# State-space block and ternary feed-forward on eight cores: 1024-wide weights cast through SBUF during the first layer norm, and the large casts issued ahead of it

## The reference, cut to what matters

```python
xn  = layernorm(x)                                   # x: 16 x 2048 x 1024, float32
xB  = einsum('bsd,nd->bsn', xn, B)                   # 128 states
state = tanh(state @ A.T + xB[:, t])                 # scan over 2048 steps
y   = einsum('bsn,dn->bsd', states, C) + D * xn + xn
attn = layernorm(y) * gamma + beta
h   = silu((xn @ w1.T) * s1) * ((xn @ w2.T) * s2)    # w1, w2: 4096 x 1024
h   = gelu((h @ h1.T) * h1s)                         # h1, h2: 4096 x 4096
h   = gelu((h @ h2.T) * h2s)
out = x + attn + (h @ w3.T) * w3s                    # w3: 1024 x 4096
```

## Time and profile before

| what | value |
|---|---|
| timed runs | 7653.4 and 8165.0 us, median 7909.2 us |
| the profiled execution, its own time | 7534.3 us |
| span of the profiled execution, slowest core | 7532.7 us |
| spans of the eight cores | 7508.8 to 7532.7 us |
| TensorE busy | 5344.8 us, 71% of the span |
| VectorE, ScalarE, GpSimd busy | 14%, 11%, 5% |
| mean granted TensorE clock | 0.93 |

### The profile page before, as it was taken

One profiled execution on the slowest core, in us unless ns is written; L12 is line 12 of the kernel. 1 busy time (PEld: TensorE's weight loads), 2 busy tenths in 40 slices (PEclk: granted clock), 3 DMA queues, 4 the chain that ended last, 5 costly groups with the idle time before them and its releaser, 6 DMA issues.

```text
span 7532.7 us, 63314 instructions; the slowest of 8 cores (7508.8 to 7532.7 us)
## 1 busy us (share of the span) xinstructions
PE 5344.8 (71%) x24252; PEld 2413.4 (32%) x24252; DVE 1079.8 (14%) x2367; ACT 815.4 (11%) x1621; POOL 372.3 (5%) x265
## 2 busy tenths in 40 slices
PE   3300004677916799779968996899699969986995
PEld 2200001233402344334433443344244424432442
DVE  4400002211093200210021003000300030012001
ACT  0000001222100100111011001110110010001010
POOL 0000000000001100110010001000200020001002
PEclk9999999899957899899989998999899989998997
DMA  1499993222323344334433443344344334433442
GB/s 54 78 111 109 109 108 74 73 96 95 140 87 109 123 151 151 118 123 151 151 112 134 151 151 106 134 151 149 103 145 151 138 114 146 151 129 115 151 151 92
DMA packets 185101, 919.75 MB, mean 122 GB/s; under 512 B 20836, under 2 KB 22117, under 8 KB 108264
## 3 DMA queue, kind: packets, MB, share of 16 engines
q1 hardware_dynamic: 158872, 739.53, 28.2%
q0 software_dynamic: 21328, 159.39, 14.0%
q10 hardware_dynamic: 4608, 16.78, 0.7%
HBM read 991.12 MB, written 109.05 MB: 146 GB/s over the span
## 4 chain that ended last, share of the span: by engine, by line
PE 57%; POOL 4%; DVE 3%; DMA 3%; issue 2%; ACT 0%; SPq 0%; DVEq 0%; POOLq 0%; ACTq 0%
PE pG L550 21%; PE pH L550 20%; PE pA L494 5%; PE pB L500 4%; PE pG L610 3%; PE pH L610 3%; DMA l1ring<-w2b 2%; POOL t1b L367 1%; POOL t2b L370 1%; POOL t1b L373 1%; POOL t2b L355 1%; PE pA L419 1%; DVE xnbt L430 1%; DVE t1b L358 1%; DVE t1b L350 0%
## 5 line engine op out<-in xcount | busy, mean ns | idle before, releaser
L550 PE MATMUL pG<-hbuf,hring 128*128 128x512 bf16 x4096 | 924.7, 382 | 5.5 <-DVE hbuf L464 3.7
L494 PE MATMUL pA<-xnbt,l1ring 128*128 128x512 bf16 x2048 | 566.0, 426 | 503.8 <-DVE hbuf L464 410.6
L550 PE MATMUL pH<-hbuf,hring 128*128 128x512 bf16 x4096 | 912.5, 379 | 2.3 <-issue 1.4
L550 PE MATMUL pG<-g1buf,hring 128*128 128x512 bf16 x4096 | 906.8, 379 | 8.0 <-ACT g1buf L528 7.8
L550 PE MATMUL pH<-g1buf,hring 128*128 128x512 bf16 x4096 | 906.8, 379 | 1.0 <-ACT hbuf L528 0.8
L419 PE MATMUL pA<-eye_s,xn_tm 128*128 128x128 f32 x256 | 57.0, 392 | 827.4 <-DVE xn_tm L407 827.4
L550 PEld LDWEIGHTS pG<-g1buf,hring 128*128 128x128 bf16 x4096 | 398.7, 98 | 490.0 <-issue 13.0
L550 PEld LDWEIGHTS pG<-hbuf,hring 128*128 128x128 bf16 x4096 | 398.8, 98 | 487.4 <-issue 26.2
L550 PEld LDWEIGHTS pH<-g1buf,hring 128*128 128x128 bf16 x4096 | 399.5, 98 | 481.3 <-issue 2.5
L550 PEld LDWEIGHTS pH<-hbuf,hring 128*128 128x128 bf16 x4096 | 395.7, 98 | 472.5 <-issue 5.4
L500 PE MATMUL pB<-xnbt,l1ring 128*128 128x512 bf16 x2048 | 519.7, 400 | 0.0
(11 more groups left out here) (91 smaller groups left out, 2401.4 us busy)
## 6 DMA issues: line engine op xcount, KB each, us to landing
hring<-h1b SPq DMA_DIRECT2D x256, 1024.0 KB, 5.0
hring<-h2b SPq DMA_DIRECT2D x256, 1024.0 KB, 5.1
l1ring<-w1b SPq DMA_DIRECT2D x256, 256.0 KB, 2.7
l1ring<-w2b SPq DMA_DIRECT2D x256, 256.0 KB, 2.9
hring<-w3b SPq DMA_DIRECT2D x64, 1024.0 KB, 5.5
xrb<-x POOLq DMA_DIRECT2D x96, 512.0 KB, 4.5
h1b<-h1t POOLq DMA_DIRECT2D x1, 32768.0 KB, 474.2
h2b<-h2t POOLq DMA_DIRECT2D x1, 32768.0 KB, 783.1
```

Of the source, the lines that this page charges most:

```text
L494: op("tensor", lambda e, p=pa, s=sl1, kk=k: e.matmul(p[:, 0:512], l1slot(s)[:, kk * 128:(kk + 1) * 128], xnbt[:, kk * 512:(kk + 1) * 512], ...
L550: op("tensor", lambda e, p=pg_, s=hs, kk=k, r=rsrc: e.matmul(p[:, 0:512], hslot(s)[:, kk * 128:(kk + 1) * 128], r[:, kk * 512:(kk + 1) * 512],
```

## The change

Three things are altered.

1. The DMAs that cast h1, h2 and w3 move from behind the phase 1 loop in GpSimd's stream to a place ahead of it, so they come before the loop's loads of `x`.
2. The DMAs that cast w1 and w2 are gone. In their place `emit_w12cast(u)` handles one of 64 pieces of 128 x 1024: SyncE loads the float32 piece to one of two halves of a new buffer `wcin`, VectorE casts it to `wcout`, and SyncE stores that to `w1b` or `w2b`. Each of the 32 iterations of the phase 1 loop ends with two such pieces.
3. SyncE's first loads from `w1b` and `w2b` wait for the 64 stores, in place of the two cast DMAs.

```diff
+        wcin = sb1("wcin", [128, 2 * 1024], F32)
+        wcout = sb1("wcout", [128, 2 * 1024], BF16)
...
         CV0_ALL = cv0.n
+
+        CSEM = {"h1": clC, "h2": clD, "w3": cv}
+        for nm_, s_, d_ in (("h1", h1t_d, h1b_d), ("h2", h2t_d, h2b_d),
+                            ("w3", w3t_d, w3b_d)):
+            op("gpsimd", lambda e, ss=s_, dd=d_: e.dma_start(dd, ss), CSEM[nm_], 16)
+
+        def emit_w12cast(u):
+            w_src = w1t_d if u < 32 else w2t_d
+            w_dst = w1b_d if u < 32 else w2b_d
+            mm_ = u % 32
+            slot = u % 2
+            ssem = cs if u < 32 else csB
+            wait("sync", cv0, CV0_CONSTS)
+            wait("sync", cl, u - 1)
+            ldn = dop("sync", lambda e, s=w_src[mm_],
+                      d=wcin[:, slot * 1024:(slot + 1) * 1024]: e.dma_start(d, s),
+                      wlc1 if slot == 0 else wlc2)
+            wait("vector", wlc1 if slot == 0 else wlc2, ldn)
+            if u >= 2:
+                wait("vector", cs if (u - 2) < 32 else csB,
+                     ((u - 2) + 1) * 16 if (u - 2) < 32 else ((u - 2) - 32 + 1) * 16)
+            cn = op("vector", lambda e, sl=slot: e.tensor_copy(
+                wcout[:, sl * 1024:(sl + 1) * 1024],
+                wcin[:, sl * 1024:(sl + 1) * 1024]), cl)
+            wait("sync", cl, cn)
+            dop("sync", lambda e, d=w_dst[mm_], sl=slot: e.dma_start(
+                d, wcout[:, sl * 1024:(sl + 1) * 1024]), ssem)
+
 
         for i in range(32):
...
             gset("pB0", (xb, xb.n))
+            emit_w12cast(2 * i)
+            emit_w12cast(2 * i + 1)
 
         gset("sqtmp", (v0b, v0b.n))
-        CSEM = {"w1": cl, "w2": clB, "h1": clC, "h2": clD, "w3": cv}
-        for nm_, s_, d_ in (("w1", w1t_d, w1b_d), ("w2", w2t_d, w2b_d),
-                            ("h1", h1t_d, h1b_d), ("h2", h2t_d, h2b_d),
-                            ("w3", w3t_d, w3b_d)):
-            op("gpsimd", lambda e, ss=s_, dd=d_: e.dma_start(dd, ss), CSEM[nm_], 16)
...
                 if tj == 0 and m == 0:
-                    wait("sync", cl, 16)
-                    wait("sync", clB, 16)
+                    wait("sync", cs, 32 * 16)
+                    wait("sync", csB, 32 * 16)
```

More of the change, by code:

```diff
@@ L136, in _build @@
                  "mmH", "scH", "mmW", "vW", "mmC2", "vC2", "mmT3",
-                 "v3", "x3", "x4", "mmF", "v7", "vout", "sout", "sdbg", "vsc", "p7")
+                 "v3", "x3", "x4", "mmF", "v7", "vout", "sout", "sdbg", "vsc", "p7", "wlc1", "wlc2")
         SM = {n: Sem(es.enter_context(nc.semaphore(n))) for n in names}
@@ L141, in _build @@
          sc2, v5b, wl, wlB, wh, mmL, scL, vL, mmH, scH, mmW, vW, mmC2,
-         vC2, mmT3, v3, x3, x4, mmF, v7, vout, sout, sdbg, vsc, p7) = (
-            SM[n] for n in names)
+         vC2, mmT3, v3, x3, x4, mmF, v7, vout, sout, sdbg, vsc, p7,
+         wlc1, wlc2) = (SM[n] for n in names)
         sbT = lambda n, shp, dt: es.enter_context(nc.sbuf_tensor(n, shp, dt))
```

## The result

The changed kernel is slower by 1.5%: the ratio to the kernel before is 1.015, with a 95% interval of 1.0099 to 1.0201. The interval excludes no change; whether 2% is reached it leaves open. Its timed runs have a median of 7669.3 us (7646.4 to 8173.2, 11 runs), those of the kernel before 7722.1 us (7533.7 to 8165.0, now 10 runs). The profiled execution took 7652.6 us, against 7534.3 before. The prediction said 7647 us.

What follows compares the result with a forecast made beforehand. It took VectorE's 751 us wait for `x`, behind five casts on GpSimd's queue, as the bound. +670.7 (later loop), +192 (pieces) and -750 (wait) gave +112.7 us on 7534.3: 7647 us, range 7580 to about 7830.

Steps and rivals of the forecast that it cites:

- The loop's start: Phase 1 loop, behind the casts and the constants: first instruction at 725 us, between 710 and 750.
- The casts: h1, h2 and w3 first in GpSimd's queue: 709 us, plus 8 for SyncE's constants beside them.
- The constants: SyncE's loads ahead of the loop, slowed by the casts: the last lands at about 691 us, against 26.1 before.
- The preparation: Between the last constant and the loop: 28 us, with row loads a few us more while the casts last.
- The pieces: Two per phase 1 iteration: 6.0 us per iteration, 192 us over 32, with bounds of 166 and 234.
- The second load's landing: End of each loop iteration, behind the first piece's store on SyncE: not hidden, 3.9 us to land.
- What goes: At `gen_a(0)`: VectorE's wait of 751 us for `x` disappears, and TensorE's transposes start at about 1288.7.
- The sum: Shift of `gen_a(0)`'s first transposes: +670.7 us from the loop's later start, +192 from pieces, -750 from the wait, +112.7 together.
- A: Second piece's load in each iteration: SyncE's round trip is longer, 7.3 us per iteration, slower by over 2%; chance 0.26.
- B: Phase 1 loop: both pieces hidden, only VectorE's casts count, 45 us; -34 us, 7500 us; chance 0.06.
- C: Loop's start: the load of `x` is not held by the casts; 7632 us; chance 0.68 together with the forecast.
- the last step: Whole kernel: the shift of +112.7 us added to the profiled execution's 7534.3 us gives 7647 us, +1.5%.

Runs made afterwards that it cites:

- f1: Kernel before with `gen_a(0)`'s loads of `x` on SyncE's queue, casts in pieces with rows of 1024 elements and waits for single pieces: 7067.8 us.

## Why the prediction was right or wrong

By the steps of the prediction, for core 3:

- *The loop's start.* The casts were put at 709 plus 8 for the company of the constants, and the load of `x` at 718. It landed at 716.6. The constants were put at 691 and landed at 698: bt took 327.5 us (319 by 65 packets of 4.9), the seven others 45 to 53 each and ones 16 (10 forecast). The preparation took 31.3 us instead of 28.2. The start was put at 725 and came at 729.3.
- *The pieces.* 6.0 us per iteration were forecast. From the start of the loop (729.3) to its end (1196.7) it took 467.4 us, so (467.4 - 279.7) / 32 = 5.9. The second load's landing was put at 3.9 us and took 3.7 in the median. The mechanism was the one named: 32 waits of VectorE for the second piece's load, 146.2 us in sum and 4.6 each, as forecast, and none for the first.
- *What goes.* The wait of 751 us is gone and nothing took its place; the load for `gen_a(0)` was there, and VectorE normalised right behind the 97th step (forecast 1287, found 1286.6).
- *The sum.* +112.7 us forecast, +111.4 measured on the same core. The ratio, 1.015, is the forecast +1.5%. That the sum is so close is in part luck: the loop began 4.3 us late, and the pieces took 187.7 us in all, 4.3 less than the 192 forecast. On another chip the loop with the casts ahead of it began at 712.4 and 720.8.
- *The rivals.* A, a round trip of over 7.2 us per iteration, did not come. B, both pieces hidden, came only with SyncE's order changed. C's premise, that the load of `x` passes the casts, is refuted by 712 us of waiting. The rule of the Trainium skill that the DMAs of all issuing engines interleave ("DMA: Bandwidth & Descriptors", "Issuing engines are not separate DMA queues") holds here for different queues: beside the casts, the loads of `x` on ScalarE's queue landed within 51.5 us, and VectorE waited 82 to 93 us for a piece on SyncE's. That section does not speak of the order within one engine's queue, so the 855 and 712 us on GpSimd's do not contradict it; the prediction was wrong to set them against it. The Trainium skill's fit (the same page, on the anatomy of one DMA), 3.2 us for 512 KB, is for GpSimd's path, where a load of `x` took 4.6; SyncE's loads of `wcin` landed in 3.4 us at least and 3.7 in the median, so here too the rows were the better guide.

What failed is the last step, from the sum to the stated time: "On the profiled execution's 7534.3 us that is 7647 us". The shift was right; the level to which it was added was not the level of the time it is compared with. The time shown for the kernel before was a median of two runs, 7909.2 us, 375 above the profiled execution. The prediction named this distance and let the top of its range allow 119 us for it, but put it at nothing in the number itself. So 7647, read beside 7909.2, says 3.3% faster, although the text says 1.5% slower; what was measured is 1.5% slower. With ten runs the median of before is 7722.1, still 188 above the profiled execution, and the fastest, 7533.7, is at its level; the median of the changed kernel, 7669.3, lies only 17 above its own profiled execution. So the two medians fall, from 7722.1 to 7669.3, where the ratio, 1.015, is a rise: the distance of a median from the profiled execution is larger than the change. That the stated 7647 lies within 0.3% of the changed kernel's median is therefore no proof of the step. A time that is to be compared with a median has to say so in the number itself, or be given as a ratio.

The bound on what a measurement can tell was also too coarse: 2% was said, and the interval came out at half a per cent to either side, which is enough to call this slower.

## What to carry to other kernels

A cast or copy of whole tensors by DMA holds back two things in different ways. What is queued behind it on the same queue waited for all of it (751 us before, 712 after). What is on another queue got through, but late: with rows of 16384 elements in the cast, a load of 256 KB took 51 to 96 us to land in the kernel before instead of 2.7, and with rows of 1024 elements 11.3 in the median. So in this kernel the row length of the big transfer set the latency of the small ones. With the long rows the wait is about one packet of the cast for each packet of the load (9 x 4.9 = 44 us for 51.3). With the short ones this count gives less than was measured (9 x 0.3 = 3 us), and what adds to it is open.

Before moving such a transfer earlier, look for what it will then stand ahead of. The gain here lay in cutting it into small rows and pieces and letting it run beside work that leaves the DMA engines idle. In a stream that runs in order, issue every load ahead of the store that has to wait for the result of another.

## What the runs showed of the hardware that was not expected

While nothing large ran beside them, the length of the rows hardly changed the speed of the casts. The pieces of w1 and w2, 2 MB in bfloat16 each, followed one another on GpSimd every 19.9 us in rows of 16384 elements (334.1 to 433.5 in five steps) and every 20.7 us in rows of 1024 (337.9 to 441.6). Two of them from each kernel's timeline of GpSimd, long rows first:

```profile
374.43 0.50 POOL L321 DMA_DIRECT2D w1b<-w1t  x1 [19.90 <-DMA w1b<-w1t]
394.31 0.50 POOL L321 DMA_DIRECT2D w2b<-w2t  x1 [19.39 <-DMA w2b<-w2t]
```

```profile
379.46 0.87 POOL L322 DMA_DIRECT2D w1b<-w1t  x1 [18.14 <-DMA w1b<-w1t]
400.97 0.87 POOL L322 DMA_DIRECT2D w2b<-w2t  x1 [20.65 <-DMA w2b<-w2t]
```

Beside SyncE's loads it was different. A piece of h1, 8 MB in bfloat16, followed the one before after 78.5 and 79.3 us with long rows, and after 103.7 and 98.3 with small ones. One issue of each, long rows first:

```profile
709.08 0.55 POOL L326 DMA_DIRECT2D h1b<-h1t  x1 [78.78 <-DMA h1b<-h1t]
```

```profile
798.68 2.03 POOL L327 DMA_DIRECT2D h1b<-h1t  x1 [96.23 <-DMA h1b<-h1t]
```

The DMA engines were full in both stretches of `gen_l1(0)` (shares of 0.97 and 0.98) and moved 118 and 128 GB/s. What the small rows gave to the other loads the casts paid for: the last one ended at 1462 us in f1 and at 1178 with long rows. How much of this is sharing and how much the rows themselves was not tried. Small rows also cost more of GpSimd's time at issue, 0.87 for 0.50 us for a piece of w1 and 2.03 for 0.55 us for one of h1, little against the waits that they remove.
